# Two broadcast rows by DMA in batches 1 and 2, and a projection product placed two half steps earlier, in a decoder block on one core

## The chip, the cores and the metric

The kernel runs on one core of a Trainium2 chip. The metric is the device time of one execution in microseconds, the median of several runs. All 16 batches are handled by this one core, in one launch.

## The reference, cut to what matters

The reference is one post-norm decoder layer over x and a context, both 16 x 512 x 512 (batch, token, channel):

```
qkv = x @ Wqkv.T + b;  q, k = elu(q*scale)+1, elu(k*scale)+1      # 16 heads of 32
y   = q * cumsum(k*v) / clip(sum_d q*cumsum(k), 1e-3)             # cumsum over tokens
x   = layernorm(x + y @ Wproj.T + bproj)
# channel attention, twice (global, local), 4 heads of 128 channels, over the 512 tokens
S   = (x*wq+bq).T @ (ctx*wk+bk) * 512**-0.5                       # 128 x 128 per head
att = softmax(S) @ (ctx*wv+bv).T
x   = layernorm(x + 2*(att_global + att_local)*wp + bp)
# one of 8 experts per batch, chosen from the mean token
x   = layernorm(x + relu(x @ W1[e] + b1[e]) @ W2[e] + b2[e])      # 512 -> 2048 -> 512
```

Two vectors of 512 numbers arise in each batch in the channel attention and are needed on all 128 partitions. The first is the sum of the context over the tokens (the "context row", for the bias terms of S). The second is the constant of the attention's output, made of the softmax weights, bv, wp and bp (the "constant row", which is added to every token). Both come into being as columns: 128 partitions x 4 numbers. To spread them to rows is what the changed constants are about.

## The kernel before, in words

All matrix products with float32 accuracy are made of three products of parts (high x high, high x low, low x high). TensorE therefore runs a very long list of 128x512 matmuls, and VectorE (DVE) and ScalarE (ACT) split the operands, evaluate the nonlinear functions and the norms.

The order is written out by hand. Time is cut into half steps: the outer loop runs over i (a batch's length) and the inner one over h, 32 half steps. A step with slot s of batch b stands at half step 32*b + s of the whole run. `plan(usual, *first)` gives the slot: the numbers behind the first one are for batches 0, 1, 2, and `usual` is for all others. Every engine walks through the same half steps with its own function `mix`, in which the pieces stand in a fixed order; an engine does its pieces strictly in that order and waits on semaphores. From half step 62 on, each even half step also holds one "up" product of the expert layer (12 matmuls), and each odd one a "down" product (12 matmuls).

The pieces that matter here:

- `JOB[j]`: the j-th projection product of a batch. j = 0 is the keys' first group of 128 channels, j = 1 the values' first group. On TensorE this is `qkv`. For batch 1, j = 0 and j = 1, the eight matmuls with the high part of x are done earlier (`ahead`, at half step 17), so that only four matmuls with the low part are left at the slot itself. One half step after the slot DVE does `keys` or `values`; `values` is one multiply and two cumulative sums (L755, L758, L759).
- `SPREAD`: batch 0 at 20 and 21. TensorE multiplies the reciprocal denominators out to all channels (`spread_reciprocal`, L1182), two groups in each half step. DVE multiplies them in with `times_reciprocal` (L803) at the same half steps, 20 and 21, and does `low_part` (L807) four times at 21. `PROJECT` of batch 0 (23 to 26) is the attention's output product, 48 matmuls (L1196 to L1198), which waits for the low parts.
- DVE's order within a half step: `keys` and `values` of the slot before come ahead of `times_reciprocal` and `low_part`.
- The context row and the constant row have two forms. Batches outside `BY_DMA` (0, 1, 2 and 15) take the matmul form: GpSimd (POOL) writes a diagonal matrix with `diagonal`, TensorE multiplies it with ones by two matmuls (`ctx_sums`, `constants`), and ACT copies the result from PSUM. In batches 1, 2 and 15 POOL then adds the constant row to x before the attention's output is added.
- Batches in `BY_DMA` (3 to 14) take the DMA form: ACT's queue stores the column to DRAM (KEEP_CSUM, KEEP_CONST) and three half steps later, after a wait for the store, loads it back to all partitions (LOAD_CSUM into `c_sb`, LOAD_CONST into `const_b`). POOL adds the constant row to tile t of x at ADD_CONST + t, after `residual2` has added the attention's output to that tile, and the norm's statistics on DVE wait for POOL's addition (`x1c_done`).
- `ATTEND` + t: TensorE's output product of the attention for tile t (8 matmuls of 128 columns, L1290), all into the same PSUM bank, so that `attend(c, t)` waits for `residual2(c, t-1)` on DVE. `residual2(c, t)` stands at ATTEND + 1 + t.

DVE's list of one half step, cut to the lines that matter:

```
for j, slot in enumerate(JOB):
    if (a := at(i, h, slot + 1)) is not None:
        ...                       # keys, values, queries
for t in range(TT):
    if (c := at(i, h, ATTEND + 1 + t)) is not None:
        residual2(c, t)
for t in range(TT):
    if (c := at(i, h, ADD_CONST + t)) is not None and c in BY_DMA:
        statistics(1, c, t)       # waits for x1c_done
for n in range(2):
    if (a := at(i, h, SPREAD + n)) is not None:
        times_reciprocal(a, 2 * n)
        times_reciprocal(a, 2 * n + 1)
```

Of the kernel before, what the change touches and what calls it, by code (L numbers as in the profile page):

```python
# [13 lines left out]
NB = 16  # L14
# [3 lines left out]
TT = T // P  # L18
# [19 lines left out]
AHEAD = 8  # L38
LAST = FC - 4
LOGITS_BY_DMA = range(2, NB - 1)  # L40
BY_DMA = range(3, NB - 1)


def upto(batch, per, n):
# [8 lines left out]
def rank(b):  # L53
    return min(b, BY_DMA.start)

# [5 lines left out]
def plan(usual, *first):  # L61
    return np.array(list(first) + [usual] * (NB - len(first)))


def at(i, h, slot):
    return next((b for b in range(max(i - 3, 0), min(i + 2, NB)) if slot[b] == HALVES * (i - b) + h), None)
# [7 lines left out]
    return None  # L74


JOB = [plan(*p) for p in ((0, 0, -12, -13), (1, 1, -10, -11), (2, 3, -5, -11), (4, 5, -3, -9), (5, 7, -1, -8), (6, 8, 0, -6), (10, 11, 2, 6), (11, 12, 2, 7), (12, 13, 4, 8), (14, 15, 5, 9), (15, 16, 8, 12), (16, 17, 9, 13))]
SPLIT_1 = plan(-1, 16)
LOAD_X = plan(17)
LOAD_CTXT = plan(18)  # L80
# [17 lines left out]
EXPS = plan(39, 36, 40)  # L98
WEIGH = plan(40, 37, 43)
TURN = plan(43, 41, 46)  # L100
KEEP_CONST = plan(42)
LOAD_CONST = plan(45)
ADD_CONST = plan(47)
CONST = plan(44, 43, 47)
ATTEND = plan(45, 43, 48)
NORM_2 = plan(51, 51, 53)
# [9 lines left out]
def build(nc, d, out):  # L116
# [4 lines left out]
    with ExitStack() as ctx:  # L121
# [3 lines left out]
        def sem(name):  # L125
            return ctx.enter_context(nc.semaphore(name))
# [95 lines left out]
        aT_mm, kb_mm, aT_done, kb_done, x1c_done = (sem(n) for n in ("aT_mm", "kb_mm", "aT_done", "kb_done", "x1c_done"))  # L222
# [73 lines left out]
        def _(sp):  # L296
# [34 lines left out]
            for i in range(NB + 3):  # L331
                for h in range(HALVES):
                    for j, slot in enumerate(JOB):
                        if (a := at(i, h, slot)) is not None:
# [59 lines left out]
        def _(pool):  # L394
# [35 lines left out]
            def tile_sum(b, done):  # L430
                x = X[b % NX]
                pool.tensor_tensor(x_sum[:, :], x[:, 0, :], x[:, 1, :], ALU.add).then_inc(done, 1)
                for t in range(2, TT):
                    pool.wait_ge(done, (TT - 1) * (b - 1) + t - 1)
                    pool.tensor_tensor(x_sum[:, :], x_sum[:, :], x[:, t, :], ALU.add).then_inc(done, 1)
# [11 lines left out]
            def mix(i, h):  # L447
# [6 lines left out]
                if (a := at(i, h, NORM_1 + 1)) is not None:  # L454
# [4 lines left out]
                    if a > 0:  # L459
                        tile_sum(a, xsum_done)  # L460
                if (c := at(i, h, WEIGH + 2)) is not None and c not in BY_DMA:
                    pool.wait_ge(kall2_done, c + 1)
# [10 lines left out]
                for t in range(TT):  # L473
                    if (c := at(i, h, ADD_CONST + t)) is not None and c in BY_DMA:
                        pool.wait_ge(const_in, 16 * (c - BY_DMA.start + 1))
                        pool.wait_ge(res2_done, TT * c + t + 1)
                        pool.tensor_tensor(X[c % NX][:, t, :], X[c % NX][:, t, :], const_b[:, :], ALU.add).then_inc(x1c_done, 1)
                if (c := at(i, h, CONST + 1)) is not None and c > 0 and c not in BY_DMA:
                    pool.wait_ge(kb_done, rank(c))
# [8 lines left out]
                if (c := at(i, h, NORM_2)) is not None:  # L488
# [4 lines left out]
                    if c > 0:  # L493
                        tile_sum(c, x2sum_done)
                if (a := at(i, h, CTX_SUM + 1)) is not None and a not in BY_DMA:
                    pool.wait_ge(csum_done, XH * a + XH)
# [16 lines left out]
        def _(act):  # L513
# [85 lines left out]
            def mix(i, h):  # L599
                if (b := at(i, h, FFN)) is not None:  # L600
                    split_x2(b, 3)
                for j, slot in enumerate(JOB):
                    if (a := at(i, h, slot)) is not None:
# [7 lines left out]
                if (c := at(i, h, LOAD_CSUM)) is not None and c in BY_DMA:  # L611
# [4 lines left out]
                                  csum_dram[c:c + 1, :].broadcast_to([P, C])).then_inc(csum_in, 16)  # L616
                if (c := at(i, h, KEEP_CONST)) is not None and c in BY_DMA:
                    act.wait_ge(kall2_done, c + 1)
                    act.dma_start(by_column(const_dram[c]), k_all2[:, :], allow_slow_non_contiguous=True).then_inc(const_st, 16)
                if (c := at(i, h, LOAD_CONST)) is not None and c in BY_DMA:  # L620
                    act.wait_ge(const_st, 16 * (c - BY_DMA.start + 1))

                    act.wait_ge(csum_done, XH * c + XH)
                    act.wait_ge(x1c_done, TT * (c - 1))
                    act.dma_start(const_b[:, :], const_dram[c:c + 1, :].broadcast_to([P, C])).then_inc(const_in, 16)
                if (c := at(i, h, CTX_ROW)) is not None and c not in BY_DMA:
                    act.wait_ge(c_mm, rank(c) + 1)
# [29 lines left out]
                if (z := at(i, h, FFN + 44)) is not None:  # L657
                    normalise(2, z)
                if at(i, h, JOB[8]) == 0:
                    act.wait_ge(made, MADE)  # L660
# [68 lines left out]
        def _(dve):  # L729
# [264 lines left out]
            def mix(i, h):  # L994
                if (b := at(i, h, FFN)) is not None:
                    split_x2(b, 3)
                if at(i, h, SCORES) == 0:
# [3 lines left out]
                                   AX.X).then_inc(experts_done, 1)  # L1001
                for j, slot in enumerate(JOB):
                    if (a := at(i, h, slot)) is not None:
                        if a == 0 and 1 <= j <= JOBS - NQ:
                            split_job(j + NQ - 1)
                for j, slot in enumerate(JOB):
                    if (a := at(i, h, slot + 1)) is not None:
# [34 lines left out]
                for t in range(TT):  # L1042
                    if (c := at(i, h, ADD_CONST + t)) is not None and c in BY_DMA:
                        statistics(1, c, t)
# [74 lines left out]
        def _(pe):  # L1119
# [258 lines left out]
            def mix(i, h):  # L1378
                if (b := at(i, h, FFN)) is not None:
                    transpose_x2(b, 3)  # L1380
                for j, slot in enumerate(JOB):
                    if (a := at(i, h, slot)) is not None:
# [115 lines left out]
```

## Time and profile before

| | |
|---|---|
| time, median of 3 runs | 2339.97 us (2337.87 to 2339.98) |
| the profiled execution's own time | 2338.21 us |
| its span in the profile | 2336.6 us |
| granted TensorE clock, mean | 0.999 |
| busy: TensorE, DVE, ACT, POOL | 99%, 69%, 49%, 16% |

The span runs from the first to the last instruction that the profiler saw; the profiled execution's time lies 1.6 us above it. Instants below are microseconds from the start of that span. A matmul of 128x512 shows about 390 ns in the profile, because its whole passage through the array is counted; one follows another much more quickly, so the distance between starts, not this number, is the cost of one.

### The profile page before, as it was taken

How to read it: one execution, taken by the hardware profiler on the slowest of the kernel's cores; microseconds unless marked ns; L12 is line 12 of the kernel's file. 1: busy time of each engine (PE TensorE's matmuls, PEld its weight loads, DVE VectorE, ACT ScalarE, POOL GpSimd, SP SyncE). 2: the span in 40 equal slices, each digit the busy share in tenths (PEclk: the TensorE clock that was granted, in tenths of full speed). 3: DMA queues.
4: the chain of work that ended last, by engine and by line, in shares of the span. 5: the costliest groups of instructions: out<-in, count | busy, mean ns of one | idle time of the engine just before them, and what ended most of it. 6: DMA issues, size and time to landing. Idle time of an engine off the chain costs nothing.

```text
span 2336.6 us, 34089 instructions
## 1 busy us (share of the span) xinstructions
PE 2315.8 (99%) x11986; PEld 1918.9 (82%) x11986; DVE 1621.2 (69%) x2876; ACT 1134.5 (49%) x1878; POOL 379.2 (16%) x323
## 2 busy tenths in 40 slices
PE   9999999999999999999999999999999999999998
PEld 7878888888888888888888888888888888888787
DVE  8876686866768667586675867758677576865643
ACT  5354544454454544545455444544454444454553
POOL 0111211121111211202112021210212102121200
PEclk9999999999999999999999999999999999999999
DMA  9355436464564635546465454654547545463332
GB/s 339 87 161 189 118 136 172 140 208 119 150 174 128 229 104 178 145 130 229 113 183 141 141 199 131 189 136 146 176 130 212 122 144 177 135 164 99 104 115 88
DMA packets 115275, 361.11 MB, mean 155 GB/s; under 512 B 26786, under 2 KB 26914, under 8 KB 104994
## 3 DMA queue, kind: packets, MB, share of 16 engines
q1 hardware_dynamic: 80210, 319.02, 40.7%
q0 software_dynamic: 16896, 33.56, 9.1%
q10 hardware_dynamic: 18000, 6.35, 1.2%
q8 instruction: 97, 1.59, 0.3%
q14 instruction: 72, 0.59, 0.1%
HBM read 335.76 MB, written 23.12 MB: 154 GB/s over the span
## 4 chain that ended last, share of the span: by engine, by line
PE 96%; DVE 2%; ACT 1%; issue 1%; POOL 0%; DMA 0%; SPq 0%; POOLq 0%; DVEq 0%; ACTq 0%
PE acc L1357 29%; PE m L1128 13%; PE h_ps L1333 10%; PE h_ps L1335 10%; PE h_ps L1334 10%; PE m L1158 7%; PE m L1196 3%; PE m L1197 2%; PE m L1198 2%; PE m L1212 2%; PE m L1290 2%; PE m L1314 1%; PE acc L1128 1%; PE m L1169 1%; PE m L1182 1%
## 5 line engine op out<-in xcount | busy, mean ns | idle before, releaser
L590 ACT ACTIVATE hid<-h_ps,b 128x512 f32<-128x512 f32 x252 | 173.6, 689 | 587.0 <-PE h_ps L1335 586.2
L1128 PE MATMUL m<-xT_hi,wq 128*128 128x512 f32 x1320 | 408.4, 391 | 0.8 <-DVE xT_lo L1087 0.8
L1357 PE MATMUL acc<-we_hi,h_hi 128*128 128x512 f32 x1008 | 401.1, 398 | 1.5 <-DVE h_lo L992 1.5
L1333 PE MATMUL h_ps<-x2T_hi,we_hi 128*128 128x512 f32 x1008 | 399.1, 396 | 2.3 <-DVE x2T_lo L976 2.3
L1357 PE MATMUL acc<-we_hi,h_lo 128*128 128x512 f32 x1008 | 393.2, 390 | 0.0
L1335 PE MATMUL h_ps<-x2T_hi,we_lo 128*128 128x512 f32 x1008 | 393.0, 390 | 0.0
L1357 PE MATMUL acc<-we_lo,h_hi 128*128 128x512 f32 x1008 | 392.9, 390 | 0.0
L1334 PE MATMUL h_ps<-x2T_lo,we_hi 128*128 128x512 f32 x1008 | 392.9, 390 | 0.0
L992 DVE TENSOR_TENSOR h_lo<-hid,h_hi 128x512 fp32r<-128x512 f32 x252 | 203.7, 808 | 256.1 <-ACT h_hi L597 256.1
L982 DVE TENSOR_TENSOR we_lo<-raw,we_hi 128x1024 fp32r<-128x1024 f32 x256 | 329.8, 1288 | 30.6 <-ACT we_hi L580 30.6
L528 ACT ACTIVATE e_f<-m,sb_qkv,scale 128x512 f32<-128x512 f32 x116 | 90.5, 780 | 480.3 <-PE m L1158 478.2
L1128 PEld LDWEIGHTS m<-xT_hi,wq 128*128 128x128 f32 x1320 | 246.8, 188 | 51.7 <-ACT xT_hi L712 1.2
L580 ACT ACTIVATE we_hi<-raw 128x1024 fp32r<-128x1024 f32 x256 | 268.0, 1047 | 11.0 <-DMA raw<-in_w 10.4
L1158 PE MATMUL m<-xT_lo,wq 128*128 128x512 f32 x660 | 257.3, 390 | 0.0
L417 POOL TENSOR_TENSOR rstd<-var_e,half 128x4 f32<-128x4 f32 x47 | 74.9, 1593 | 1019.2 <-DVE var_e L828 1018.9
L1333 PEld LDWEIGHTS h_ps<-x2T_hi,we_hi 128*128 128x128 f32 x1008 | 189.4, 188 | 43.3 <-issue 4.0
L1357 PEld LDWEIGHTS acc<-we_hi,h_hi 128*128 128x128 f32 x1008 | 189.5, 188 | 41.1 <-issue 3.0
L1357 PEld LDWEIGHTS acc<-we_hi,h_lo 128*128 128x128 f32 x1008 | 189.3, 188 | 40.1
L1335 PEld LDWEIGHTS h_ps<-x2T_hi,we_lo 128*128 128x128 f32 x1008 | 189.3, 188 | 39.9
L1334 PEld LDWEIGHTS h_ps<-x2T_lo,we_hi 128*128 128x128 f32 x1008 | 189.5, 188 | 37.2
L1357 PEld LDWEIGHTS acc<-we_lo,h_hi 128*128 128x128 f32 x1008 | 189.7, 188 | 36.5
L597 ACT ACTIVATE h_hi<-hid 128x512 fp32r<-128x512 f32 x252 | 159.4, 633 | 8.0
(262 smaller groups left out, 3282.1 us busy)
## 6 DMA issues: line engine op xcount, KB each, us to landing
raw<-in_w SPq DMA_DIRECT2D x256, 512.0 KB, 4.4
wq<-wq_scratch SPq DMA_DIRECT2D x168, 512.0 KB, 3.8
x<-in_x_tok SPq DMA_DIRECT2D x16, 1024.0 KB, 5.7
x<-in_b_proj POOLq DMA_DIRECT2D x16, 1024.0 KB, 14.0
ctx_T<-in_ctxT SPq DMA_DIRECT2D x16, 1024.0 KB, 9.4
x<-in_b POOLq DMA_DIRECT2D x16, 1024.0 KB, 11.5
ctx_tok<-in_ctx_tok SPq DMA_DIRECT2D x15, 1024.0 KB, 4.8
out_dram<-x SPq DMA_DIRECT2D x15, 1024.0 KB, 4.8
```

The costliest lines, as they stand in the source:

```text
L528: act.activation(e_f[:, :], ps[:, :], ACT.Exp, bias=sb_qkv[:, col:col + 1], scale=scale[:, 0:1]).then_inc(done, 1)
L580: act.activation(we_hi[:, g % NW, :], raw[:, g % NR, :], ACT.Copy).then_inc(whi_done, 1)
L590: act.activation(hid[:, f % 2, :], up_bank(b, f)[:, :], ACT.Relu, bias=b1[:, b % 2, f:f + 1]).then_inc(h_done, 1)
L597: act.activation(h_part(h_hi, xT_hi, b, f), hid[:, f % 2, :], ACT.Copy).then_inc(hhi_done, 1)
L982: dve.tensor_tensor(we_lo[:, g % NW, :], raw[:, g % NR, :], we_hi[:, g % NW, :].bitcast(F32), ALU.subtract).then_inc(wlo_done, 1)
L992: dve.tensor_tensor(h_part(h_lo, xT_lo, b, f), hid[:, f % 2, :], h_part(h_hi, xT_hi, b, f).bitcast(F32), ALU.subtract).then_inc(hlo_done, 1)
L1128: pe.matmul(bank(a, j)[:, :], w[:, s, t, :], x_hi[:, t, :], start=(t == 0 and s == 0), stop=False)
L1158: last = pe.matmul(bank(a, j)[:, :], w[:, 0, t, :], x_lo[:, t, :], start=False, stop=(t == CC - 1))
L1333: pe.matmul(ps, we_hi[:, g % NW, js], x2T_hi[:, j, :], start=(j == 0), stop=False)
L1334: pe.matmul(ps, we_hi[:, g % NW, js], x2T_lo[:, j, :], start=False, stop=False)
L1335: last = pe.matmul(ps, we_lo[:, g % NW, js], x2T_hi[:, j, :], start=False, stop=(j == CC - 1))
L1357: last = pe.matmul(acc[t][:, :], hx[:, f % 2, ts], wx[:, g % NW, C:], start=(f == 0 and n == 0), stop=(f == FC - 1 and n == 2))
```

## The change

`BY_DMA` now begins with batch 1, so that batches 1 and 2 spread both rows through DRAM as batches 3 to 14 do. Batch 1 attends three half steps later than the usual batch, so its slots for the constant row are shifted by three too. The wait for `x1c_done` in front of the first load of a constant row is left out, since no addition was made before it. Besides, the slot of batch 1's second projection product (j = 1, values) goes from -10 to -12, that is from half step 22 to half step 20; on TensorE it then stands ahead of batch 0's first `spread_reciprocal`, and DVE's `values` goes from half step 23 to 21.

```
-BY_DMA = range(3, NB - 1)
+BY_DMA = range(1, NB - 1)
 
-JOB = [plan(*p) for p in ((0, 0, -12, -13), (1, 1, -10, -11), (2, 3, -5, -11), ...
+JOB = [plan(*p) for p in ((0, 0, -12, -13), (1, 1, -12, -11), (2, 3, -5, -11), ...
 
-KEEP_CONST = plan(42)
-LOAD_CONST = plan(45)
-ADD_CONST = plan(47)
+KEEP_CONST = plan(42, 42, 45)
+LOAD_CONST = plan(45, 45, 48)
+ADD_CONST = plan(47, 47, 50)
 
                     act.wait_ge(csum_done, XH * c + XH)
-                    act.wait_ge(x1c_done, TT * (c - 1))
+                    if c > BY_DMA.start:
+                        act.wait_ge(x1c_done, TT * (c - 1))
                     act.dma_start(const_b[:, :], const_dram[c:c + 1, :].broadcast_to([P, C])).then_inc(const_in, 16)
```

## Rows read from the trace of the kernel before

**Rows 1.** The page's chain of work that ended last, shares by engine.

```profile
PE 96%; DVE 2%; ACT 1%; issue 1%; POOL 0%; DMA 0%; SPq 0%; POOLq 0%; DVEq 0%; ACTq 0%
```

**Rows 2.** Timeline of TensorE, 45 to 54 us: start, length, what, count [idle before].

```profile
45.23 1.20 PE L1158 MATMUL acc<-x2T_lo,wq 128*128 128x512 f32 x4
48.69 0.73 PE L1182 MATMUL m<-rden_all,head_all 128*128 128x512 f32 x2 [2.25 <-ACT rden_all L679]
50.15 1.10 PE L1182 MATMUL m<-rden_all,head_all 128*128 128x512 f32 x2 [0.73 <-DVE ctx_tok L803]
51.09 1.87 PE L1158 MATMUL acc<-x2T_lo,wq 128*128 128x512 f32 x4
53.24 0.77 PE L1196 MATMUL m<-wp_hi,xT_hi 128*128 128x512 f32 x1 [0.28 <-DVE xT_lo L807]
```

**Rows 3.** Timeline of DVE, 49 to 58 us.

```profile
49.42 1.28 DVE L803 TENSOR_TENSOR ctx_tok<-ctx_tok,m 128x512 f32<-128x512 f32 x2
50.61 0.69 DVE L747 SCALAR_TENSOR_TENSOR k_sum<-e_f,r_f 128x512 f32<-128x512 f32 x1
51.21 1.28 DVE L803 TENSOR_TENSOR ctx_tok<-ctx_tok,m 128x512 f32<-128x512 f32 x2
52.41 2.49 DVE L807 TENSOR_TENSOR xT_lo<-ctx_tok,xT_hi 128x512 fp32r<-128x512 f32 x4
54.82 0.74 DVE L755 SCALAR_TENSOR_TENSOR kv_sum<-acc,b_qkv,k_sum 128x512 f32<-128x512 f32 x1
...
57.85 0.67 DVE L841 TENSOR_TENSOR x<-m,x 128x512 f32<-128x512 f32 x1
```

**Rows 4.** Windows: stretch, length, busy by engine, then granted clock (PEclk), DMA.

```profile
51.00:51.50 0.50, 0.50 (x3) 0.36 (x3) 0.50 (x2) 0.36 (x1) 0.00 (x0) 0.61 1.04 426
...
54.50:55.00 0.50, 0.50 (x3) 0.42 (x3) 0.50 (x2) 0.50 (x2) 0.00 (x0) 0.97 0.12 49
```

**Rows 5.** Windows from one batch's gram product to the next: batches 2 to 3, 3 to 4.

```profile
280.37:422.06 141.69, 141.69 (x731) 117.64 (x730) 103.28 (x175) 72.00 (x120) 30.59 (x24) 1.00 0.54 159
422.06:565.51 143.45, 143.45 (x739) 119.14 (x738) 99.95 (x178) 70.03 (x116) 23.05 (x18) 1.00 0.52 158
```

**Rows 6.** TensorE's waits between 80 and 150 us: total, times, longest.

```profile
PE h_ps L1333 <- DVE x2T_lo L976: 1.0, 1, 1.0
```

**Rows 7.** The page's DMA issues: count, size, median us to landing.

```profile
c_sb<-csum_scratch ACTq DMA_DIRECT2D x12, 256.0 KB, 4.1
...
csum_scratch<-c_col ACTq DMA_DIRECT2D x12, 2.0 KB, 9.6
```

**Rows 8.** Timeline of ACT around half steps 59 to 63.

```profile
137.97 1.06 ACT L580 ACTIVATE we_hi<-raw 128x1024 fp32r<-128x1024 f32 x1 [1.40 <-DMA raw<-in_w]
...
149.53 0.63 ACT L597 ACTIVATE h_hi<-hid 128x512 fp32r<-128x512 f32 x1
```

**Rows 9.** Line L619, the store of the constant row (const_scratch<-k_all), 12 times.

```profile
DMA to landing us min/median/max: 9.8/10.4/12.4
```

**Rows 10.** Line L625, the load of the constant row (const_b<-const_scratch), 12 times.

```profile
DMA to landing us min/median/max: 5.2/6.1/7.6
```

**Rows 11.** Timeline of ACT, half steps 77 and 80 of the run.

```profile
203.59 0.77 ACT L529 ACTIVATE r_f<-m,sb_qkv,scale 128x512 f32<-128x512 f32 x1
...
215.65 0.69 ACT L590 ACTIVATE hid<-h_ps,b 128x512 f32<-128x512 f32 x1 [4.01 <-PE h_ps L1335]
```

**Rows 12.** Timeline of DVE, half steps 82 and 83.

```profile
217.64 0.68 DVE L848 TENSOR_TENSOR x<-m,x 128x512 f32<-128x512 f32 x1
...
218.97 1.21 DVE L982 TENSOR_TENSOR we_lo<-raw,we_hi 128x1024 fp32r<-128x1024 f32 x1
220.16 0.69 DVE L848 TENSOR_TENSOR x<-m,x 128x512 f32<-128x512 f32 x1
```

**Rows 13.** Timeline of TensorE, batch 1's last attention tile (half step 83).

```profile
222.70 1.05 PE L1290 MATMUL m<-aT,ctx_T 128*128 128x128 f32 x8
```

**Rows 14.** Line L477, POOL's addition of the constant row: ns min/median/max; who waited for it.

```profile
L477 POOL TENSOR_TENSOR x<-x,const_b x48: 1282/1290/1304, 487.1 to 2080.0; 128x512 f32<-128x512 f32 x48
...
  DVE stats L816: 7.8, 7
```

More of the change, by code:

```diff
@@ L74, in step @@
     return None
-JOB = [plan(*p) for p in ((0, 0, -12, -13), (1, 1, -10, -11), (2, 3, -5, -11), (4, 5, -3, -9), (5, 7, -1, -8), (6, 8, 0, -6), (10, 11, 2, 6), (11, 12, 2, 7), (12, 13, 4, 8), (14, 15, 5, 9), (15, 16, 8, 12), (16, 17, 9, 13))]
+JOB = [plan(*p) for p in ((0, 0, -12, -13), (1, 1, -12, -11), (2, 3, -5, -11), (4, 5, -3, -9), (5, 7, -1, -8), (6, 8, 0, -6), (10, 11, 2, 6), (11, 12, 2, 7), (12, 13, 4, 8), (14, 15, 5, 9), (15, 16, 8, 12), (16, 17, 9, 13))]
 SPLIT_1 = plan(-1, 16)
```

## The prediction, made before the changed kernel ran

> **What bounds the kernel now.** I read the chain of waits first, because it says which engine has to be made faster. TensorE holds 96% of it [rows 1]: from the first product to the last the matmuls stand one behind another, and the time is the number of matmuls by their distance plus the few places where TensorE waits. So there are only two questions: how many matmuls go away, and at which places TensorE waits longer or less than now. The second view is therefore TensorE's timeline at the place that the moved product leaves and enters. It shows a hole: after the four low matmuls of batch 1's first product (45.23) TensorE is idle 2.25 us until ACT has laid out the reciprocals, runs two spread matmuls at 48.69, is idle 0.73 us for DVE, runs the other two at 50.15, then the four matmuls of the second product at 51.09, and starts batch 0's output product at 53.24 after a last 0.28 us for DVE's low part [rows 2]. The third view is DVE's timeline beside it: DVE has no idle time there at all. It multiplies two groups (49.42), does batch 1's keys (50.61), the other two groups (51.21), the four low parts (52.41), and only then the values of batch 1 (54.82 to 57.85) [rows 3]. The start of the output product at 53.24 is the first low part (52.41 and 0.6 us) and the handing over. It is DVE's order that sets it, not TensorE's work: the second product is done in time in which TensorE would have waited anyway. Last, the windows by batch and the rows of the two DMA round trips price the other half of the change.
>
> **Part 1: eight matmuls go.** Per batch the matmul form takes two for the context row and two for the constant row; with batches 1 and 2 that is eight. Their distance comes from two windows: from the gram product of batch 2 to that of batch 3 there are 731 matmuls in 141.69 us, in the next 739 in 143.45 us. The first has the four row matmuls and lacks twelve of a down product. 1.76 us for 8 is 0.22 us each [rows 5]. Eight are 1.8 us. The same two windows are a test of the DMA form in itself: with twelve more and four fewer the second would take 143.45 if no wait was added, and TensorE was busy in the whole of it (143.45 of 143.45). The DMA form costs TensorE nothing in batch 3, whose slots batch 2 has. Term: -1.8 us, with batch 2 clean. POOL's diagonals and ACT's copies go too and ACT's queue gets four issues per batch; neither engine is on the chain (POOL and ACT hold 0 and 1% of it) [rows 1], so I cost this at nothing. What covers it is TensorE's backlog of matmuls; without it an issue would cost the ACT time of a third of a microsecond.
>
> **Part 2: the product moves up.** On TensorE its four matmuls (0.9 us) fill a part of the 2.25 us hole, and at 51.09 nothing stands in their place. That gains nothing, since the output product waits for DVE. On DVE `values` moves from behind the low parts to between the keys and the second pair of multiplications. Its own input is ready by then (TensorE is through with it at about 47.4), so it runs at 51.2 and takes what it took, 54.82 to 57.85, 3.0 us [rows 3]. The second pair, the low parts and with them the output product start 3.0 us later, at about 56.3. No instruction of TensorE can fill the time from 51.3 to 56.3, since all that follows stands behind the output product. Afterwards DVE has 3.0 us less to do behind the low parts, but there it has nothing to give back: its next work is the residual of the output product (57.85), which is TensorE's follower. Term: +3.0 us. Bounds: nothing less than that is possible unless the delay is caught up later (a rival, below).
>
> **The clock.** The granted clock was 0.61 in the mean of 51.00 to 51.50 and 0.97 in that of 54.50 to 55.00 [rows 4]. With the two levels 1.0 (2.4 GHz) and 0.50 (1.2 GHz) this means that it fell at 51.1 and rose at 54.5, so it stood at half for 3.4 us; before the fall TensorE had been idle for 3.0 of 4.6 us, before the rise it had worked almost throughout. Of this the output product felt 53.24 to 54.5, which cost half of it, 0.65 us. Afterwards TensorE is idle for 5 us just ahead of the output product, so I let it start at half speed and stay there for one such stretch of 3.4 us, which costs 1.7 us; the difference is +1.0 us. Bounds: -0.7 (it never stands at half there) and +2.7 (two stretches). The Trainium skill, TensorE: Matmul & The Clock Gate, in "What's actually happening", says that the throttled clock is the default state and that activity releases it; this speaks against a move that closes one hole and opens a longer one right before 48 matmuls, and the fall behind a hole in this trace agrees.
>
> **Part 3: are the two rows there in time in batch 1?** Context row: ACT's queue comes to the store behind the split that ends at 139.0, and to the load three half steps later behind the copy that ends at 150.2 [rows 8]. The store takes 9.6 us in the median and the load 4.1 [rows 7], so the wait for the store (until 148.6) is over when ACT arrives, and the row is there at about 154, while DVE takes it only six half steps behind the load. Cost: nothing; the cover is those six half steps, and without them the load's 4.1 us would stand open. Constant row: ACT comes to the store behind the copy that ends at 204.4 [rows 11]. It lands 10.4 us later, at 214.8 (9.8 to 12.4) [rows 9]. ACT has by then come to the load, and what stands behind its wait is the hidden layer's copy, which waits until 215.65 itself [rows 11]; so the median store is covered by 0.9 us and the longest would delay that copy by 1.2 us, which the down product three half steps later doesn't feel. The load takes 6.1 us in the median, 5.2 to 7.6 [rows 10], while a load of the same size took 4.1 [rows 7]. Between the two medians I take 5.1: it lands at 219.9, and POOL's first addition of 1.3 us [rows 14] ends at 221.2. At half step 82 DVE's statistics of tile 0 wait for it. Behind them stand a split of weights (1.2 us) and then the residual of tile 2, which is now done at 220.8 [rows 12] and which TensorE's last attention tile waits for. From the end of the addition it is 0.1 for the signal, 0.6 for the statistics, 1.2 for the split, 0.7 for the residual: 223.8. TensorE comes there at 222.70 [rows 13], less 0.4 for the two matmuls of the constant row just before, so at 222.3. It waits 1.5 us. From batch 3 on the same order costs DVE a wait in 7 of 12 batches (7.8 us in all) [rows 14] and TensorE none that the chain shows, but there a projection product stands between the attention tiles; in batch 1 there is none at these half steps. Bounds of this term: the short end is 0 (store 9.6 and load 4.1 give 222.0), the long end (12.4 and 7.6) gives 228.3 and a wait of 6.0. Term: +1.5 us. After it the tiles follow TensorE, and the norm's half step comes later by as much.
>
> The Trainium skill, DMA: Bandwidth & Descriptors, in "Anatomy of one DMA", gives a DMA about 2.0 us and its bytes over 436 GB/s; by that store and load would take 2.0 and 2.6 us, the row would be there before anyone asks, and the sum would be 1.5 us lower. These rows show a store of 2 KB at 9.6 us and more, so I go by them. The same page's table of advice says that a strided last dimension becomes one descriptor per element, which fits a small store that is slow.
>
> **The sum.** -1.8 + 3.0 + 1.0 + 1.5 = +3.7 us. On the profiled execution's own time of 2338.21 (1.6 us over its span of 2336.6) this is 2341.9. The median of the runs is 2339.97, and two of the three lie within 0.01 of it, and the profiled one is 1.8 below them; I put the difference on the median: 2343.7 us. A difference of 0.2%, 4.7 us, is about what can be told from none; the forecast stays under it, narrowly.
>
> **The rivals.** (a) The late constant row decides, and the kernel is slower. The place is the statistics of tile 0 in batch 1. If the store lands at its longest and the load at 6.1 or more, TensorE waits 4.5 to 6 us instead of 1.5, and the sum is +6.7 to +8.2; it decides, that is the sum passes +4.7, from a wait of 2.5 us on, which is reached with the load's own median of 6.1. For it: two medians in a row suffice, and two stretches at half clock (+1.7) have the same effect. Against it: the DMA queues' load differs in batch 1, and c_sb's 4.1 us shows that such a load can be quick. Taken as +4.7 to +8.2, middle +6: 2346. (b) The delay is caught up. Between 80 and 150 us TensorE waits six times for DVE or ACT, none over 1.0 us [rows 6], and if these waits were set by work that doesn't stand behind the output product, up to 4 us could vanish in them; the row might also be there in time. Then the sum is between -2.5 (the matmuls and a clock that stays up) and +1, in the middle -0.8: 2339.2. Against it: DVE idles for TensorE behind the output product, so its later work hangs on TensorE and moves along. (c) The move does what its place suggests and more than the matmuls is gained. The idle times around the hole are 3.3 us in all [rows 2] and the matmuls 1.8; only both in full, 5.1 us, would pass 4.7. (d) That `values` doesn't in fact come ahead of the second pair: the order of the list says otherwise.
>
> **How the numbers follow.** Forecast, +1 to +4.7: 0.56, of which a small part would reach just over the bound. Slower by (a): 0.26. Caught up (b): 0.14. Faster by (c): 0.03, and the remainder on the slow side. That makes faster by over 0.2% 0.03, within 0.2% 0.66, slower 0.31. The range for 8 in 10 leaves out the lower half of (b) and the upper third of (a): 2339.6 to 2347.3 (-0.4 to +7.3).
>
> **What would show it.** In the changed kernel's timelines: the second product's four matmuls right behind the first's and the hole before the first spread at about 1.3 us instead of 2.25; on DVE a line L755, L758, L759 between L747 and the second L803; the first L1196 at 56 and a hole of about 5 us in front of it, with a granted clock of 0.50 behind it. In batch 1: a store from ACT's queue near 208, a load near 218, POOL's first L477 at about 223 (all shifted by the 4 us), a DVE wait in front of L816, and an idle time of 1 to 2 us before the last L1290. In the window from batch 2 to 3: four matmuls fewer and about 140.8 us. I am wrong if the output product doesn't start later, if TensorE's waits before 150 us shrink by what was lost, or if the wait in batch 1 is far from 1.5.

## The result, and the profile of the changed kernel

| | before | after |
|---|---|---|
| time, median of 6 runs each | 2339.44 us (2337.87 to 2339.98) | 2348.35 us (2347.28 to 2351.32) |
| ratio | | 1.0039, 95% interval 1.0028 to 1.005 |
| the profiled execution: time, span | 2338.21, 2336.6 | 2347.28, 2345.7 |
| granted TensorE clock, mean | 0.999 | 0.996 |

The change costs 8.9 us, 0.39%, where +3.7 us was forecast and +7.3 was the end of the range. Lines behind L625 stand one further down in the changed kernel (L1290 is L1291).

The first view is again the page's chain of work that ended last; beside [rows 1] TensorE has given up 3 points.

```profile
PE 93%; DVE 2%; issue 1%; ACT 1%; DMA 1%; POOL 0%; SPq 0%; POOLq 0%; DVEq 0%; ACTq 0%
```

The second is the list of TensorE's waits over the whole run: total, times, longest. The first two lines are new in these sizes, and they are the two places that the prediction named.

```profile
PE m L1197 <- DVE xT_lo L808: 5.2, 1, 5.2
PE m L1291 <- DVE x L849: 3.8, 3, 2.0
```

I then followed one instruction of TensorE after another through both timelines; the differences of their starts, after less before, tell where the time goes:

| TensorE comes to | before | after | difference |
|---|---|---|---|
| batch 0's output product | 53.24 | 56.21 | +3.0 |
| batch 0's first attention tile | 102.69 | 107.85 | +5.2 |
| batch 1's gram product | 148.98 | 154.12 | +5.1 |
| batch 1's attention tiles, the first | 211.82 | 216.03 | +4.2 |
| the second | 215.45 | 221.82 | +6.4 |
| the third | 219.07 | 227.17 | +8.1 |
| the fourth | 222.70 | 231.82 | +9.1 |
| batch 2's gram product | 280.21 | 289.43 | +9.2 |
| the end of the span | 2336.6 | 2345.7 | +9.1 |

So there are two losses: 5.2 us at 49 to 62 us, and 4.9 us between batch 1's first and fourth tile. Between them the difference shrinks by the four matmuls that batch 1 has lost (5.1 to 4.2) and by nothing else; before 150 us nothing is caught up. What batch 2's four matmuls save is given back in batch 3 (below).

**The first place.** TensorE and then DVE of the changed kernel, the answer to [rows 2] and [rows 3]:

```profile
45.00 2.11 PE L1159 MATMUL acc<-x2T_lo,wq 128*128 128x512 f32 x8
48.45 0.73 PE L1183 MATMUL m<-rden_all,head_all 128*128 128x512 f32 x2 [1.35 <-ACT rden_all L680]
49.92 1.10 PE L1183 MATMUL m<-rden_all,head_all 128*128 128x512 f32 x2 [0.73 <-DVE ctx_tok L804]
56.21 0.76 PE L1197 MATMUL m<-wp_hi,xT_hi 128*128 128x512 f32 x1 [5.19 <-DVE xT_lo L808]
```

```profile
51.17 0.75 DVE L756 SCALAR_TENSOR_TENSOR kv_sum<-acc,b_qkv,k_sum 128x512 f32<-128x512 f32 x1
51.95 1.23 DVE L759 TENSOR_TENSOR_SCAN k_sum<-k_sum 128x512 f32<-128x512 f32 x1
53.09 1.20 DVE L760 TENSOR_TENSOR_SCAN kv_sum<-kv_sum 128x512 f32<-128x512 f32 x1
54.21 1.26 DVE L804 TENSOR_TENSOR ctx_tok<-ctx_tok,m 128x512 f32<-128x512 f32 x2
55.38 2.49 DVE L808 TENSOR_TENSOR xT_lo<-ctx_tok,xT_hi 128x512 fp32r<-128x512 f32 x4
```

The eight matmuls stand together and the hole is 0.9 us shorter, as predicted; `values` runs from 51.17 on, the second pair is at 54.21 instead of 51.21, and the output product stands behind a hole of 5.19 us. Windows of the changed kernel (stretch, length, busy by engine, granted clock, DMA) for [rows 4]:

```profile
51.00:52.00 1.00, 0.02 (x1) 0.00 (x0) 0.86 (x3) 0.13 (x1) 0.00 (x0) 0.93 0.97 401
...
58.00:60.00 2.00, 2.00 (x6) 1.55 (x5) 0.00 (x0) 0.97 (x4) 0.76 (x3) 0.50 0.59 115
...
62.00:63.00 1.00, 1.00 (x6) 0.83 (x5) 0.97 (x2) 0.00 (x0) 0.00 (x0) 0.95 0.01 0
```

With levels of 1.0 (2.4 GHz) and 0.50 (1.2 GHz) the clock fell at 51.9 and rose at 62.1. It fell 0.9 us into the hole of 5.19 us. The output product ran at half from 56.2 to 62.1, 5.9 us, which cost 2.9 us; 0.65 was paid before, so this is +2.3.

**The second place.** ACT of the changed kernel at half steps 77 to 81, answering [rows 11]:

```profile
207.59 0.42 ACTq L619 DMA_DIRECT2D const_scratch<-k_all  x1
...
218.85 1.06 ACT L580 ACTIVATE we_hi<-raw 128x1024 fp32r<-128x1024 f32 x1 [3.98 <-DMA raw<-in_w]
218.91 0.33 ACTq L626 DMA_DIRECT2D const_b<-const_scratch  x1
219.86 0.69 ACT L590 ACTIVATE hid<-h_ps,b 128x512 f32<-128x512 f32 x1
```

The store goes out at 207.59, near the 208 predicted, and the load at 218.91, near 218. But ACT had not stood still for the store: it waited 3.98 us for a load of weights (`raw`), which SP's queue had issued at 208.1, half a microsecond behind the store. Line L389, the two weight loads of 207.9 to 213 us, changed kernel:

```profile
L389 SPq DMA_DIRECT2D raw<-in_w x2: 343/343/343, 208.1 to 212.4; - x2
...
  ACT we_hi L580: 4.6, 2
...
DMA to landing us min/median/max: 9.4/10.1/10.7
```

and the same line in the kernel before, 203 to 209 us:

```profile
DMA to landing us min/median/max: 3.2/3.6/4.0
```

Behind the late weights stand the split on DVE and behind it the residual that the second attention tile needs. DVE, then POOL:

```profile
219.94 1.23 DVE L983 TENSOR_TENSOR we_lo<-raw,we_hi 128x1024 fp32r<-128x1024 f32 x1 [4.34 <-ACT we_hi L580]
221.08 0.68 DVE L849 TENSOR_TENSOR x<-m,x 128x512 f32<-128x512 f32 x1
...
227.47 0.69 DVE L817 BATCH_NORM_STATS2 stats<-x 128x6 f32<-128x512 f32 x1 [3.46 <-POOL x L477]
228.08 3.09 DVE L983 TENSOR_TENSOR we_lo<-raw,we_hi 128x1024 fp32r<-128x1024 f32 x1
231.09 0.68 DVE L849 TENSOR_TENSOR x<-m,x 128x512 f32<-128x512 f32 x1
```

```profile
226.15 1.28 POOL L477 TENSOR_TENSOR x<-x,const_b 128x512 f32<-128x512 f32 x1 [66.77 <-DMA const_b<-const_scratch]
```

And TensorE's last three tiles of batch 1 (the rows between them are left out), with the clock after the first wait:

```profile
221.82 1.47 PE L1291 MATMUL m<-aT,ctx_T 128*128 128x128 f32 x8 [2.00 <-DVE x L849]
227.17 1.05 PE L1291 MATMUL m<-aT,ctx_T 128*128 128x128 f32 x8
231.82 1.16 PE L1291 MATMUL m<-aT,ctx_T 128*128 128x128 f32 x8 [0.83 <-DVE x L849]
```

```profile
222.00:224.00 2.00, 2.00 (x11) 1.80 (x12) 1.04 (x2) 0.84 (x1) 0.00 (x0) 0.63 0.98 372
224.00:226.00 2.00, 2.00 (x6) 1.58 (x5) 0.01 (x1) 0.00 (x0) 0.00 (x0) 0.52 0.74 298
```

Three parts make the 4.9 us: the wait of 2.00 (+2.2 with what surrounds it), the half clock that follows it (+1.7), and the wait of 0.83 (+1.0), which is the one that the prediction had priced at 1.5. That last one is the late row proper: POOL starts at 226.15, DVE's statistics wait 3.46 us for it, and the split behind them then takes 3.09 us instead of 1.23, beside POOL's next addition (228.24 to 230.07). The trace of before had such a split too, in batch 3; DVE, then POOL:

```profile
495.37 1.99 DVE L982 TENSOR_TENSOR we_lo<-raw,we_hi 128x1024 fp32r<-128x1024 f32 x1
```

```profile
494.99 1.28 POOL L477 TENSOR_TENSOR x<-x,const_b 128x512 f32<-128x512 f32 x1 [5.33 <-DVE x L848]
```

The split is longer than 1.23 by about the time that it has beside the addition: 0.8 us for 0.9 there, 1.9 for 1.8 here.

These three parts say where the 4.9 us lie on TensorE; they aren't three causes. When the last tile starts follows from the row's path alone: the load is issued at 218.91 and takes 7.2 us, POOL adds until 227.4, then come DVE's statistics, the split until 231.1 and the residual until 231.8. Without the wait before the second tile and without the half clock (222.5 to 225.9) TensorE would have come to the last tile earlier and waited there until the same 231.82. The late weights hold up this path by 0.5 us only, since the store itself had landed at 218.4 (207.59 and 10.8 us) and ACT issued the load at 218.91.

### The profile page after: what moved, and what is told of

It reads as the page before. It is cut to its first block, busy times and chain, and to the rows that moved or that the text cites. A ratio compares the mean times of both kernels' runs of the same rounds, so it can differ in the third digit from the quotient of the medians.

```text
span 2345.7 us, 34055 instructions
## 1 busy us (share of the span) xinstructions
PE 2317.9 (99%) x11978; PEld 1919.1 (82%) x11978; DVE 1613.5 (69%) x2876; ACT 1133.9 (48%) x1874; POOL 369.2 (16%) x311
## 4 chain that ended last, share of the span: by engine, by line
PE 93%; DVE 2%; issue 1%; ACT 1%; DMA 1%; POOL 0%; SPq 0%; POOLq 0%; DVEq 0%; ACTq 0%
PE acc L1358 28%; PE m L1129 13%; PE h_ps L1334 10%; PE h_ps L1336 9%; PE h_ps L1335 9%; PE m L1159 6%; PE m L1197 3%; PE m L1198 3%; PE m L1199 3%; PE m L1213 2%; PE m L1291 2%; PE m L1315 1%; PE acc L1129 1%; PE m L1170 1%; PE m L1183 1%
## 5 line engine op out<-in xcount | busy, mean ns | idle before, releaser
L993 DVE TENSOR_TENSOR h_lo<-hid,h_hi 128x512 fp32r<-128x512 f32 x252 | 204.0, 810 | 247.0 <-ACT h_hi L597 247.0
```

The costliest lines, as they stand in the source:

```text
L993: dve.tensor_tensor(h_part(h_lo, xT_lo, b, f), hid[:, f % 2, :], h_part(h_hi, xT_hi, b, f).bitcast(F32), ALU.subtract).then_inc(hlo_done, 1)
```

## The experiments

All times are medians beside runs of the kernel before on the same chip; each ratio has its 95% interval. The kernel before itself ran between 2337.8 and 2342.0 in these jobs, so an effect under 1 us is not seen in a median, but its place is seen in a trace.

A trace is one execution, and the clock at batch 0's output product is not the same in each. Of the output product 1.3 us ran at half in the profiled execution of the kernel before; in those of the six experiments below that leave the product at its old place and the hole unfilled it was 0.1, 0.4, 1.8, 1.8, 5.0 and 5.1 us. Half of that is the cost, so 0 to 2.6 us. Differences in this term between two traces have to be read with that in mind.

**The move alone, the rows alone.** In the kernel before:

```diff
-(1, 1, -10, -11)
+(1, 1, -12, -11)
```

> The kernel before with only the moved product (half step 20 instead of 22), all rows in the old form. Theory A (DVE's values push back the low parts and a long hole puts the output product at half clock): the first matmul of batch 0's output product starts at 56.2 instead of 53.2, the matmuls after it stand at half clock for about 6 us, and the whole is 5.0 to 5.4 us slower than before, as much as the changed kernel had lost by its first gram product. Rival (the move is free or helps, and all of the 9 us come from the rows through DRAM): within 1 us of before.

Measured: 2343.81 against 2339.46, ratio 1.0019 (1.001 to 1.0028), +4.4 us. TensorE of this run:

```profile
55.82 0.76 PE L1196 MATMUL m<-wp_hi,xT_hi 128*128 128x512 f32 x1 [4.90 <-DVE xT_lo L807]
```

The start is 2.6 us later than before (in this execution the first spread was 0.6 us earlier, at 48.06), and the clock stood at half from 49.6 to 59.8. Of the output product 4.0 us ran at half, which makes +1.4; about 6 us had been expected, and the expected loss of 5.0 to 5.4 us was too high.

And in the changed kernel the other way round, the rows as changed and the product back:

```diff
-(1, 1, -12, -11)
+(1, 1, -10, -11)
```

> The changed kernel with the moved product put back to half step 22; batches 1 and 2 through DRAM. Theory B (the store of batch 1's constant row holds up the weight load issued behind it, ACT, DVE and TensorE follow, the constant row itself comes late, and the clock falls once more): 3.5 to 4.5 us slower than before, with two waits of TensorE before batch 1's attention tiles. Rival (the late row was only a consequence of where the move had shifted DMA traffic): 1 to 2 us faster than before, by the eight matmuls.

Measured: 2343.04 against 2339.46, 1.0017 (1.0008 to 1.0027), +3.6 us. TensorE's second and fourth tile:

```profile
217.11 1.16 PE L1291 MATMUL m<-aT,ctx_T 128*128 128x128 f32 x8 [1.93 <-DVE x L849]
...
227.69 1.16 PE L1291 MATMUL m<-aT,ctx_T 128*128 128x128 f32 x8 [3.05 <-DVE x L849]
```

The two halves nearly add up (8.0 of 8.9), and neither needs the other: the wait for the weights is there with batch 1 at its old time as well. Eight matmuls are 1.8 us fewer in this run, so the constant row costs about 5.4 us here, not 1.5.

The clock went another way here. It stayed up after the wait of 1.93 and fell only behind that of 3.05:

```profile
222.00:224.00 2.00, 2.00 (x10) 1.68 (x9) 0.62 (x2) 0.00 (x0) 1.95 (x2) 1.00 0.03 10
...
230.00:232.00 2.00, 2.00 (x12) 1.48 (x5) 1.95 (x4) 0.00 (x0) 1.27 (x1) 0.50 0.72 132
```

It stood at half from 229.3 for 3.4 us. TensorE waited for nothing more of batch 1 behind that, so it cost 1.7 us in full: the difference to the kernel before is +5.0 at the last tile and +6.7 at batch 2's gram product.

**Which row, which batch.** In the kernel before:

```diff
-BY_DMA = range(3, NB - 1)
+BY_DMA = range(2, NB - 1)
```

> Only batch 2 joins the DMA form, batch 1 keeps the matmul form, and the product is not moved. Theory B (all of the rows' loss is batch 1's): between 1.0 us faster (four matmuls) and 0.2 us slower, since the changed kernel lost 0.8 us again at batch 3's spread. Rival (each batch in the DMA form costs): 1.5 us slower or more.

Measured: 2338.32 against 2339.46, 0.9995 (0.9986 to 1.0004), -1.1 us. And with the two rows told apart, each place that asked for `BY_DMA` asking for its row's own:

```diff
-BY_DMA = range(3, NB - 1)
+ROW_DMA = range(1, NB - 1)      # context row
+CONST_DMA = range(3, NB - 1)    # constant row
```

> Only the context row goes through DRAM from batch 1 on, the constant row does so from batch 3 as before, and the product is not moved. Theory B (the constant row alone is late): four matmuls fewer and no new wait, 0.5 to 1.2 us faster than before. Rival (any small store to DRAM at these half steps holds the weight loads up enough to stall TensorE): 1 us slower or more.

Measured: 2338.14 against 2339.46, 0.9995 (0.9986 to 1.0004), -1.3 us. Each has four matmuls fewer (0.9 us) and no loss. Everything that is lost by the rows is the constant row of batch 1; batch 2 and the context row are as free as predicted. Neither is a proven gain.

**The hole: the order on DVE.** The move alone, with DVE's own slot for `values` left where it was:

```diff
+DVE_JOB = [slot.copy() for slot in JOB]
+DVE_JOB[1][1] = -10
-                for j, slot in enumerate(JOB):
+                for j, slot in enumerate(DVE_JOB):
```

> The kernel before with the product's four matmuls at half step 20 on TensorE, but DVE's values left at half step 23. Theory A (the loss of the move is DVE's order alone): the output product starts at 53 to 53.5 as before, and the time is within 0.7 us of before, a little slower if the emptier hole keeps the clock at half for longer behind it (up to 1.7 us). Rival (the place on TensorE costs as well): as slow as the move alone, 4.4 us over before.

Measured: 2340.63 against 2339.64, 1.0003 (0.9994 to 1.0012), +1.0 us.

```profile
53.39 0.77 PE L1198 MATMUL m<-wp_hi,xT_hi 128*128 128x512 f32 x1 [1.70 <-DVE xT_lo L809]
```

The output product is back at 53.4: the 3.0 us were DVE's `values` and nothing else. What is left in this trace is the clock, which stood at half until about 57.7 (4.3 us of the output product at half are 2.2, less 0.65: +1.5). In the kernel before the four matmuls kept TensorE at work just ahead of the output product; where they stand now, they do not. That this is why the clock stayed down longer is not shown: with the product at its old place two executions had 5.0 and 5.1 us at half.

**The hole: the clock.** The move alone, with twenty float32 products of the all-ones matrix in front of the output product (the trace counts each as two):

```diff
+                if i == 0 and h == 22:
+                    keep_busy(M2, 20)
```

> The move alone, and 20 matmuls of ones into an unused bank at half step 22, in the hole ahead of batch 0's output product; they add nothing to any result. Theory A (3.0 us of the move's 4.4 are the wait and the rest is the clock): the output product starts at 56 as in the move alone, now at full clock, and the time is 2.0 to 3.0 us over before. Rival (no part of the loss is the clock's): still 4.4 us over before.

Measured: 2341.15 (2340.59 to 2342.21) against 2339.64, 1.0007 (0.9998 to 1.0016), +1.5 us, 2.9 less than the move alone.

```profile
50.40 4.63 PE L1122 MATMUL m<-ones 128*128 128x128 f32 x40
55.75 0.48 PE L1196 MATMUL m<-wp_hi,xT_hi 128*128 128x512 f32 x1 [0.73 <-DVE xT_lo L807]
```

```profile
54.00:56.00 2.00, 1.27 (x11) 1.11 (x10) 2.00 (x4) 1.56 (x3) 0.00 (x0) 1.00 0.04 16
```

The start is as late as in the move alone (55.75), and the clock never falls. +2.5 for the start and -0.65 for the half clock that the kernel before pays make +1.9; +1.5 was measured.

**The store in other pieces.** The rows alone, the store of the constant row written as 128 pieces of 16 bytes instead of 512 of 4. The row then comes back permuted, and this kernel leaves out putting it in order, so its output is not the reference's:

```diff
-act.dma_start(by_column(const_dram[c]), k_all2[:, :], ...)
+act.dma_start(const_dram[c].rearrange("(p h) -> p h", h=XH), k_all2[:, :])
```

> The rows through DRAM without the move, but the store of the constant row writes each partition's four numbers side by side (128 pieces of 16 bytes instead of 512 of 4), so the row comes back in a permuted order and the output differs from the reference. Theory B (the store in 512 pieces holds the DMA engines): the store lands in 5 us or less instead of 10.7, the weight loads behind it in 4 to 5 instead of 10.4, TensorE's first wait (1.9 us) goes, the row is there in time, and the whole is 0.5 to 1.8 us faster than before. Rival (any store to DRAM with a load behind it takes that long): as the rows without the move, 3.6 us slower.

Measured: 2336.44 against 2339.64, 0.9988 (0.9979 to 0.9997), -3.2 us. The two weight loads behind the store, and the load of the row:

```profile
L389 SPq DMA_DIRECT2D raw<-in_w x2: 343/343/343, 202.3 to 206.6; - x2
...
DMA to landing us min/median/max: 3.3/3.7/4.2
```

```profile
213.25 1.28 POOL L477 TENSOR_TENSOR x<-x,const_b 128x512 f32<-128x512 f32 x1 [59.73 <-DMA const_b<-const_scratch]
```

Beside the rows alone, the store lands in 3.4 us instead of 10.7, the weights in 3.7 instead of 10.4, POOL starts at 213 instead of 222, and TensorE waits before no attention tile of batch 1. The same bytes by the same queues at the same place: it is the form of the store that makes the weights late. It makes the row late at the same time. This run and the ones below change both together, so what the late weights would have cost TensorE with the row in time was not measured. The gain is more than the 1.8 us of the eight matmuls and more than was expected; the clock explains 0.6 of it in the profiled execution (0.1 us of the output product at half), the rest was not followed. How the small pieces hold back a transfer of another queue is not shown. The windows of the changed kernel show only that little moves while the loads are outstanding: 6, 23, 41 and 55 GB/s in the four stretches of 2 us from 212 to 220.

**The store earlier.** The rows alone, in batch 1 one half step earlier:

```diff
-KEEP_CONST = plan(42, 42, 45)
-LOAD_CONST = plan(45, 45, 48)
+KEEP_CONST = plan(42, 42, 44)
+LOAD_CONST = plan(45, 45, 47)
```

> The rows through DRAM without the move, with batch 1's constant row stored one half step earlier (slot 44) and loaded one earlier (47). Theory B (a store that starts at about 197 instead of 203 is through before the weight load of half step 79 is issued at 203.5): both waits before the attention tiles go or shrink to under 1 us, 0.5 to 1.8 us faster than before. Rival (the late row is not the binding wait): 3 us slower or more.

Measured: 2338.65 against 2339.64, 0.9996 (0.9987 to 1.0005), -1.0 us. The store still takes 9.4 us and the weights 7.8 in the median, but both are late at a place with more room; TensorE's waits before the tiles are 0.55 and 0.74. One half step is worth 4.6 us. The expected reason was not the one found: the store went out at 197.8 and landed at 207.2, behind the issue of the weight load at 204.0, which still took 9.3 us.

**A usable form of the fast store.** As above with the contiguous store, and POOL reads `const_b` in the row's order:

```diff
-const_b[:, :]
+const_b[:, :].rearrange("p (q h) -> p h q", h=XH)
```

> The store of e7_contiguous_store (128 pieces of 16 bytes) with the row put in order where it is used: GpSimd's additions of const_b read it with a step of four elements. Nothing of the computation is left out. If the slow part of the constant row is the store in 512 pieces alone, this is as fast as e7: 2336.4 us against 2339.6 for the kernel before, so a ratio near 0.9986; the weight loads of half step 79 land in 3 to 4 us, and TensorE has no wait of over 1 us before the attention tiles of batch 1. If GpSimd's addition pays for the step of four elements (it takes 1.3 to 1.8 us now), and DVE waits for it before its statistics, up to 4 us of e7's gain goes: 2336 to 2340.

Measured: 2337.47 against 2339.44, 0.9992 (0.9983 to 1.0001), -2.0 us. Line L477 in this run:

```profile
L477 POOL TENSOR_TENSOR x<-x,const_b x56: 1526/1554/2058, 215.2 to 2079.5; 128x512 f32<-128x512 f32 x56
```

An addition takes 1.55 us instead of 1.29 and TensorE does not feel it: its only wait for a residual in the run is 0.9 us. This computes all of the reference and is 5.6 us faster than the rows alone with the slow store, relative to the kernel before. Whether it beats the kernel before is at the edge of what was measured. (Its profiled execution was one of those with a long half clock, 5.1 us of the output product.)

**The same with the hole of the kernel before filled**, by eight products of ones:

```diff
+                        if a == 0 and n == 0:
+                            keep_busy(M2, 8)
                         spread_reciprocal(a, 2 * n)
```

> e9_contiguous_read_permuted with eight fp32 products of the all-ones matrix (128 columns, about 1.9 us by the 4.63 us of twenty) ahead of batch 0's spread of the reciprocals, where TensorE idles 2.25 us in the kernel before. Their result is not used. If the clock before the output product of batch 0 is held up by them, the half clock of 51.0 to 54.5 us, which costs about 0.65 us, is gone and the runs spread less: 2335.7 us, up to 2 us below e9 on chips where the clock falls earlier. If it falls anyway, nothing changes: 2336.4. If the products run past the releaser of the spread they cost up to 0.5 us.

Measured: 2337.47 against 2339.44, 0.9991 (0.9982 to 1.0), the same median as without the eight products, so nothing gained. In the profiled execution, which at 2341.80 was the slowest of the eleven, the clock fell nevertheless:

```profile
52.00:54.00 2.00, 1.35 (x4) 0.66 (x3) 2.00 (x4) 1.68 (x4) 0.00 (x0) 0.50 0.88 373
```

It fell at 51.9 and rose at 58.8. In the two stretches of 2 us ahead of the fall TensorE had been at work for 1.34 and 1.36 us: the products of ones end before the spread, and the idle places behind them stayed. Three of the eleven executions (2336.59 to 2337.79) have a mean granted clock of 1.000, which none of the kernel before beside them has (0.998 and 0.999), so the fall may have been absent or shorter there; they aren't faster than the others, and no trace of them was taken. So the 0.65 us of the kernel before were not won back by this, and what would do it is open.

## Why the prediction was wrong, step by step

- **"Part 1: eight matmuls go", -1.8.** Right. It shows at batch 1's attention (5.1 becomes 4.2 at the first tile) and in the experiments on single rows (-1.1 and -1.3 for four matmuls each).
- **"Batch 2 clean".** Its slots were: the difference at its attention tiles is +8.3, after +9.2 at its gram product. But the 0.9 us came back: TensorE waits 0.66 us for ACT's reciprocals at 378.7 in the changed kernel, where ACT had itself waited 0.81 us for POOL's `shift`. From gram to gram it takes 141.72 us, not the 140.8 predicted. The runs with the rows alone and with the fast store have no such wait. It was not followed further.
- **"Part 2: the product moves up", +3.0.** Right to 0.1 us: 56.21 against "about 56.3", and the experiment with `values` left late takes nearly all of it away (53.39 against 53.24).
- **"The clock", +1.0 (bounds -0.7 to +2.7).** The mechanism was right, and in the profiled execution the term was too small: +2.3. I had let the half clock last for one stretch of 3.4 us as in [rows 4]; it lasted 10.2 us, of which 5.9 were in the output product. One fall's length is no measure of another's, not even in the same arrangement: the move alone had 4.0 us of the output product at half (+1.4), and with the product at its old place the seven profiled executions had 0.1 to 5.1. So the size of this term in one trace is partly luck. That the hole's clock costs something is not: filling it took 2.9 us off the move alone, median against median, each beside the kernel before. The rule of the Trainium skill that was cited (TensorE: Matmul & The Clock Gate, "What's actually happening": the clock is throttled by default and activity releases it) agrees with the run with the filled hole: TensorE stayed at work and the clock stayed up.
- **"Part 3", context row at nothing.** Right: load issued at 154.7, landed in 7.2 us, first used at 166.9.
- **"Part 3", constant row +1.5 (0 to 6.0). This is the step that failed.** It measured +4.9 in the changed kernel. The row's path to the last tile was the right one, and the last tile waited for it; three of its lengths were wrong. The load took 7.2 us where I had taken 5.1 (+2.1). The split between the statistics and the residual took 3.1 us where I had taken 1.2 (+1.9), as I had read it from [rows 12], where POOL adds nothing beside it. The store took 10.8 instead of 10.4 and ACT issued the load 0.5 us behind its landing (+0.9); against this, the store went out 1.4 us earlier than I had read it from [rows 11] (203.0 in the rows alone, not 204.4). Together that is about the 3.4 by which the term was off. Why the load took 7.2 us is not shown; in the run with the contiguous store it took 4.6.

  The second thing that was wrong is what I left out: the other work in the DMA system beside the store. I had written that ACT's queue "waits until 215.65 itself", and had counted a late copy for ACT as something "which the down product three half steps later doesn't feel". But the weight load issued half a microsecond behind the store took nearly three times as long, and ACT, DVE's split, DVE's residual of tile 0 and TensorE's second tile were all queued behind it. This put a wait of 2.0 us at a place where I had none, and the clock fell behind it. In the changed kernel both lie inside the time that the last tile would have waited for the row anyway; with the row in time they would have stood alone, about 2.2 us and up to 1.7 for the clock, an estimate from the tiles above. The half clock is a cost that the prediction had counted only at the first place, and in the rows alone it came behind the last wait and cost 1.7 us on top.

  The estimate of the Trainium skill that was set beside these terms (DMA: Bandwidth & Descriptors, "Anatomy of one DMA") is fitted there to DMAs that GpSimd issues, and these go out on ACT's queue; its 2.0 and 2.6 us stand against 10.8 and 7.2 measured.
- **The rows that would have told** are in the trace of before. One is the split of 1.99 us beside an addition, shown above. The other is line L389, the weight load issued at 470.3 us, behind batch 3's store of the constant row:

```profile
DMA to landing us min/median/max: 9.9/9.9/9.9
```

  It costs nothing there: it lands at 480.2, and ACT takes these weights at 481.14, when it comes to them. I had read the landing times of the two DMAs that the change adds and never those of the DMAs issued next to them. "The DMA form costs TensorE nothing in batch 3" was a statement on that batch's slack, not on the form.
- **The rivals.** (a), the late constant row decides, came nearest: its place and its path were right, and its wait of 4.5 to 6 us holds the 4.9. It had put the length into the store, where it was in the load and the split. Its +4.7 to +8.2 falls short by 0.7, as more half clock at the first place (+1.3) and the 0.7 us given back in batch 3 came on top. (b), caught up: wrong, the six waits of [rows 6] stayed at 1.0 us and less. (c) and (d): wrong.
- **The range** ended at +7.3. At the first place the clock alone was 1.3 above the forecast and at the second the constant row 3.4; the bounds of the two terms (+2.7 and +6.0) held each of them, but the range did not reach to where both are in their upper half; the 0.7 us given back in batch 3 come on top.

## What to carry to other kernels

A DMA in many small pieces isn't only slow itself: look in the trace for what is issued behind it, on any queue, and whether that is wanted soon. Where such a transfer is already in the kernel, the landing times of its neighbours there give the price. The row that is itself being moved must be followed with the lengths that its steps have beside the other engines' work, such as the split beside POOL's addition. And a wait that opens on TensorE can have a second term, the half clock around it: 2.9 us in the output product behind the wait of 5.2, 1.7 us behind that of 3.05 in the rows alone. It came after some waits of 2 us and not after others, and it costs only where TensorE has nothing to wait for behind it: behind the wait of 2.00 in the changed kernel it lay inside the wait for the row. In a sum it is a bound, not a fixed term.

## What the runs showed of the hardware that was not expected

- 2 KB from 128 partitions to DRAM took 10.0 to 12.7 us (median 11.4) in 512 pieces of 4 bytes, and 3.3 to 3.5 us in 128 pieces of 16 bytes (the changed kernel and the run with the contiguous store, 14 stores each). Loads of 512 KB issued behind it on another queue took 9.4 and 10.7 us instead of 3.2 and 4.0.
- The granted clock stood at half for 10.2 us around a hole of 5.2 us; the last 5.9 us were filled with matmuls back to back. After the wait of 2.0 us in batch 1 it stood at half for 3.4 us (0.63 and 0.52 in the windows of 222 to 226 us), and after the wait of 1.93 us at the same place in the rows alone it stayed at 1.00.
- The same part of the program ran at half clock for different lengths in different executions: 0.1 to 5.1 us of batch 0's output product with the product at its old place.
- DVE's split of 128x1024 took 3.1 us instead of 1.2 while POOL added rows in the same stretch (3.09 in the changed kernel, 3.05 with the rows alone), and 2.0 us where 0.9 us of an addition fell beside it (batch 3 of the kernel before).
- POOL's addition of 128x512 with one operand read at a step of four elements took 1.55 us against 1.29.
